# A recurrent mixing layer's preparation and scan, reordered by step, with the state held in PSUM

## What is computed

```
xx = shift(x) - x;  mix = x + xx*maa_x;  lo = tanh(mix @ w1) (4 groups);  xm[g] = x + xx*(lo[g] @ w2[g] + maa[g])
r, k, v, g, w2, kk, a, ma, mk = small projections of xm[0..3], some through tanh or sigmoid
w = -softplus(-(decay + w2)) - 0.5;  kk = k + ..., normalized per head
k = k*(ma + a*(1-ma)) * exp(w*mk);   b = -kk*a;   w = exp(-exp(w))
per head, per step:  s = s*w + (s @ kk)*b + v*k;   y = s @ r
y = groupnorm(y)*ln_w + ln_b + (r*k*faaaa summed per head)*v;   out = (y*g) @ Wo
```

## Time and profile before

| | us |
|---|---|
| median of 3 runs | 2137.53 (2132.94 to 2140.84) |
| the profiled execution, its own time | 2134.84 |
| its span, first to last instruction | 2132.8 |
| `build_projections` | 0 to 69.1 |
| `build_gates` | 69.1 to 166.7 |
| `build_scan` | 166.7 to 336.4 |
| `build_mix_output` | 336.4 to about 450 |
| the six layers and the end | to 2132.8 |

### The profile page before, as it was taken

The page is one execution under the profiler, slowest core; times in us unless marked ns, Lnnn a source line. Parts: engine busy times, 40 slices in busy tenths (PEclk is TensorE's granted clock), DMA queues, the critical chain, the costliest instruction groups (busy, mean ns, idle before and its releaser), DMA issues. The chain is left out here.

```text
span 2132.8 us, 74062 instructions
## 1 busy us (share of the span) xinstructions
PE 1907.6 (89%) x31300; PEld 1318.9 (62%) x31300; DVE 1569.4 (74%) x2888; ACT 1221.0 (57%) x2361; POOL 1161.1 (54%) x682
## 2 busy tenths in 40 slices
PE   6576777948999999999999999999999999999984
PEld 2113556825677766667776776766777677776662
DVE  4768997347787787777877778777787777877743
ACT  4500001126677676776766767667677676776751
POOL 1401221018667666666666767666676666766630
PEclk9788998559999999999999999999999999999996
DMA  1000000033222222322223222232222322322220
GB/s 56 0 0 1 1 0 20 1 128 72 66 67 68 65 72 65 111 66 64 72 69 110 69 64 72 71 105 67 67 72 74 102 68 64 73 63 62 69 53 20
DMA packets 84859, 128.49 MB, mean 60 GB/s; under 512 B 26736, under 2 KB 32304, under 8 KB 83504
## 3 DMA queue, kind: packets, MB, share of 16 engines
q1 hardware_dynamic: 84528, 123.75, 22.8%
HBM read 21.94 MB, written 1.05 MB: 11 GB/s over the span
## 5 line engine op out<-in xcount | busy, mean ns | idle before, releaser
L961 POOL TENSOR_TENSOR qk<-qk,rnorm 128x1024 f32<-128x1024 f32 x192 | 361.4, 1904 | 368.9 <-ACT rnorm L1186 292.6
L955 POOL TENSOR_TENSOR qk<-qk,turnedhalf 128x1024 f32<-128x1024 f32 x192 | 454.8, 2369 | 142.8 <-DVE turnedhalf L1312 142.8
L1308 DVE TENSOR_TENSOR qk<-bank,gains 128x512 f32<-128x512 f32 x384 | 262.2, 683 | 235.1 <-ACT squares L1176 220.6
L1012 PE MATMUL bank<-wqkv,x 128*128 128x512 f32 x768 | 377.8, 595 | 22.0 <-DMA qk_gain<-in_qk_gain 20.1
L1176 ACT ACTIVATE squares<-bank 128x512 f32<-128x512 f32 x384 | 232.6, 606 | 166.0 <-PE bank L1012 163.2
L1312 DVE TENSOR_TENSOR turnedhalf<-bank,gains 128x256 f32<-128x256 f32 x768 | 285.3, 412 | 0.0
L1223 ACT ACTIVATE o_T<-bank 128x512 f32<-128x512 f32 x192 | 104.3, 599 | 229.7 <-PE bank L1076 229.6
L1318 DVE TENSOR_REDUCE rnorm<-squares 128x16 f32<-128x1024 f32 x192 | 230.6, 1201 | 2.8
L1076 PEld LDWEIGHTS bank<-p_T,v_win 64*64 64x64 f32 x12288 | 189.8, 135 | 58.0 <-issue 57.7
L1025 PEld LDWEIGHTS bank<-st_ident,qk 128*128 128x128 f32 x1536 | 179.0, 142 | 58.3 <-issue 52.2
L1017 PE MATMUL bank<-wqkv,x 128*128 128x512 f32 x384 | 202.0, 607 | 7.2 <-DVE turnedhalf L1312 6.7
(11 more groups left out here) (200 smaller groups left out, 3080.9 us busy)
## 6 DMA issues: line engine op xcount, KB each, us to landing
v_win<-v_tok SPq DMA_DIRECT2D x1536, 64.0 KB
wqkv<-in_wqkv SPq DMA_DIRECT2D x6, 1536.0 KB
wo<-in_wo SPq DMA_DIRECT2D x6, 512.0 KB
w<-in_w SPq DMA_DIRECT2D x6, 341.0 KB
w<-in_w SPq DMA_DIRECT2D x6, 192.0 KB
xT_sb<-in_xT SPq DMA_DIRECT2D x1, 1024.0 KB, 5.7
x_tok_sb<-in_x_tok SPq DMA_DIRECT2D x1, 1024.0 KB, 4.8
tables<-in_tables SPq DMA_DIRECT2D x2, 512.0 KB, 4.5
```

Source lines behind the costliest of these rows:

```text
L955: nc.gpsimd.tensor_tensor(out=qk[n % 2][:, half], in0=qk[n % 2][:, half], in1=turnedhalf[:, half], op=ALU.add).then_inc(rot_added.sem, 1)
L961: nc.gpsimd.tensor_tensor(out=by_head(qk[u][:, half]), in0=by_head(qk[u][:, half]), in1=rnorm[u][:, AH * i:AH * (i + 1)].unsqueeze(2).to_b ...
L1012: nc.tensor.matmul(QK_BANKS[i][:, :], shifted_tokens(x, n, P), layer_cols(wqkv, n, 3 * INNER, 512 * i, 512), start=True, stop=True).then_i ...
L1308: nc.vector.tensor_tensor(by_head(qk[u][:, cols]), src, cos.to_broadcast([P, 8, DH]), ALU.mult).then_inc(rotated.sem, 1)
```

## The change

The whole mixing layer is done in step order: the host lays x out by step, so that every tensor of the first phase is already in the order in which the scan reads it. `build_gates` is gone as a phase.

- The projections wait for only three loads first (xT, vecs, w_lo) and for the others before the fifth product. `spread` is no longer loaded. v is projected first in each group, written to DRAM, and read back by SyncE with each row repeated over the 8 rows of its head (16 DMAs for a group of 512, 2 MB in SBUF). GpSimd sums the decays along the steps with 31 additions of 128 x 64. VectorE makes the gain of k by group, with a second sigmoid on ScalarE for 1 - a. g is written turned into token order by ScalarE.
- The rest of the gates' work is made for one group of 8 steps (128 x 512) at a time. Group 0 comes ahead of the first step; groups 1 to 3 are spread as `stages` over the steps of the group before, 9 operations on VectorE, 10 on ScalarE and one product on TensorE for each group. Much of it stays in two PSUM banks, `KK_BANK` and `Z_BANK`.
- The states lie in PSUM banks 4 and 5 and are renewed in place. VectorE makes both products with r out of PSUM. vk is made step by step by GpSimd, two steps ahead (`times_k`), and added by GpSimd to half 0's product with b (`add_vk`); VectorE's `renew0` adds that sum to the state.
- In `build_mix_output` the bonus (line 599) is written turned into token order.

The diff, cut to its core:

```diff
...
-        MAA, FIRST = ("maa0", "maa1", "maa2", "maa3"), ("r", "g1", "xwa", "k", "xk", "v")
-        SECOND = ("g2", "z", "a", "ma", "kk", "mk")
+        MAA, FIRST = ("maa0", "maa1", "maa2", "maa3"), ("v", "r", "g1", "xwa", "k", "xk")
+        SECOND = ("kk", "a", "mk", "ma", "z", "g2")
...
+            for name in FIRST_LOADS:
+                sp.dma_start(t[name][:, :], a[name]).then_inc(loaded_first.sem, 16)
+            for name in rest:
+                sp.dma_start(t[name][:, :], a[name]).then_inc(loaded.sem, 16)
+            for j in range(GROUPS):
+                sp.wait_ge(v_made.sem, j + 1)
+                sp.dma_start(v_dram[:, g_of[j]], t["v"][:, g_of[j]]).then_inc(v_stored.sem, 16)
+                if j == 0:
+                    sp.wait_ge(v_stored.sem, 16)
+                    for h in range(HEADS):
+                        rows = slice(HS * h, HS * (h + 1))
+                        sp.dma_start(v_rep[rows, :, :, :].rearrange("p i l c -> p i (l c)"),
+                                     v_dram[rows, g_of[0]].unsqueeze(0).to_broadcast([HS, HS, GROUP])).then_inc(v_copied.sem, 16)
+            sp.wait_ge(v_stored.sem, 16 * GROUPS)
+            sp.wait_ge(v_copied.sem, 16 * HEADS)
...
+                at, end = max(GROUP * j, CHUNKS), GROUP * (j + 1)
+                nc.vector.tensor_tensor(xx[:, at:end], xT[:, at - CHUNKS:end - CHUNKS], xT[:, at:end], ALU.subtract).then_inc(xx_made.sem, 1)
+                dve.wait_ge(xx_made.sem, 2 * B + j + 1)
...
+                for g in (3, 0, 1, 2):
...
+            def gain(j):
+                gain_j = unheld[:, g_of[j]]
+                dve.wait_ge(a_made.sem, a_made.after(j))
+                dve.wait_ge(ma_made.sem, ma_made.after(j))
+                nc.vector.tensor_tensor(gain_j, gain_j, ma[:, g_of[j]], ALU.mult).then_inc(gain_step.sem, 1)
+                dve.wait_ge(gain_step.sem, gain_step.after(j, 1))
+                nc.vector.tensor_tensor(gain_j, gain_j, t["a"][:, g_of[j]], ALU.add).then_inc(gain_step.sem, 1)
+                dve.wait_ge(gain_step.sem, gain_step.after(j))
+                dve.wait_ge(kk_made.sem, j + 1)
+                nc.vector.tensor_tensor(t["k"][:, g_of[j]], t["k"][:, g_of[j]], gain_j, ALU.mult).then_inc(k_gained.sem, 1)
...
+            def sums(j):
+                pool.wait_ge(z_made.sem, z_made.after(j))
+                for l in range(max(STEPS * j, 1), STEPS * (j + 1)):
+                    if l > 1:
+                        pool.wait_ge(summed.sem, l - 1)
+                    w = [t["w"][:, CHUNKS * m:CHUNKS * (m + 1)] for m in (l - 1, l)]
+                    nc.gpsimd.tensor_tensor(out=w[1], in0=w[0], in1=w[1], op=ALU.add).then_inc(summed.sem, 1)
...
+                    nc.scalar.activation(unheld[:, g_of[j]], bank("a", j)[:, :], ACT.Sigmoid, scale=-1.0,
+                                         bias=vecs[:, V_NAAAAA:V_NAAAAA + 1]).then_inc(a_made.sem, 1)
...
+                    out = t["g"][:, :].rearrange("p (c l) -> p l c", l=CHUNK)[:, STEPS * j:STEPS * (j + 1), :]
+                    nc.scalar.activation(out, bank("g2", j)[:, :].rearrange("p (l c) -> p l c", c=CHUNKS), ACT.Copy).then_inc(g_made.sem, 1)
...
+        def in_step(l, stages):
+            j, s = (l + STEPS) // STEPS, l % STEPS
+            if j < GROUPS:
+                for stage in stages[s]:
+                    stage(j)
...
+            squares(0)
+            absolutes(0)
+            log_z(0)
+            inverse_norm(0)
+            decays(0)
+            key_gain(0)
+            growths(0)
+            decays_again(0)
+            stages = ((squares, absolutes), (log_z, inverse_norm), (decays,), (), (), (key_gain,), (growths,), (decays_again,))
...
+            def renew0(l):
+                if l:
+                    dve.wait_ge(vk_added.sem, l + 1)
+                    nc.vector.tensor_tensor(S_BANKS[0][:, :], S_BANKS[0][:, :], ubvk[:, :], ALU.add).then_inc(s_new[0].sem, 1)
+                else:
+                    dve.wait_ge(vk_made.sem, 1)
+                    nc.vector.tensor_copy(rows(S_BANKS[0][:, :]), vk_of(0)).then_inc(s_new[0].sem, 1)
+            def renew1(l):
+                dve.wait_ge(ub_made[1].sem, l + 1)
+                nc.vector.tensor_tensor(S_BANKS[1][:, :], S_BANKS[1][:, :], ub[:, 1, :], ALU.add).then_inc(s_new[1].sem, 1)
+            def times_r(p, l):
+                dve.wait_ge(s_new[p].sem, l + 1)
+                dve.wait_ge(r_made.sem, l // STEPS + 1)
+                if l >= 2:
+                    dve.wait_ge(y_product.sem, y_product.after(l - 2))
+                nc.vector.tensor_tensor(m2[:, l % 2, :, p, :], rows(S_BANKS[p][:, :]), step(r_step, l), ALU.mult).then_inc(s_r[p].sem, 1)
...
+            soft_sum(0)
+            soft_gate(0)
+            soft_growth(0)
+            unit_kk(0)
+            steps_a(0)
+            times_a(1, 0)
+            gated_kk(0)
+            steps_k(0)
+            steps_b(0)
+            steps_r(0)
+            stages = ((), (), (soft_sum, unit_kk), (soft_gate, gated_kk), (soft_growth, steps_a), (steps_k,), (steps_b,), (steps_r,))
+            for l in range(CHUNK):
+                if l:
+                    times_b(0, l)
+                times_b(1, l)
+                renew1(l)
+                if l + 1 < CHUNK:
+                    times_a(1, l + 1)
+                renew0(l)
+                if l + 1 < CHUNK:
+                    times_a(0, l + 1)
+                times_r(1, l)
+                times_r(0, l)
+                in_step(l, stages)
...
+            def times_k(l):
+                j = l // STEPS
+                pool.wait_ge(k_made.sem, j + 1)
+                if j:
+                    pool.wait_ge(v_copied.sem, v_copied.after(j - 1))
+                nc.gpsimd.tensor_tensor(out=vk_of(l), in0=vk_of(l), in1=step(k_step, l), op=ALU.mult).then_inc(vk_made.sem, 1)
+            def add_vk(l):
+                pool.wait_ge(ub_made[0].sem, l)
+                pool.wait_ge(vk_made.sem, l + 1)
+                if l >= 2:
+                    pool.wait_ge(s_new[0].sem, l)
+                nc.gpsimd.tensor_tensor(out=rows(ubvk[:, :]), in0=rows(ub[:, 0, :]), in1=vk_of(l), op=ALU.add).then_inc(vk_added.sem, 1)
+            for l in range(AHEAD):
+                times_k(l)
+            pool.wait_ge(s_new[0].sem, 1)
+            pool.sem_inc(vk_added.sem, 1)
+            for l in range(CHUNK):
+                if l:
+                    add_vk(l)
+                if l + AHEAD < CHUNK:
+                    times_k(l + AHEAD)
...
-            times_a(0, 0)
-            add_vk(0)
-            times_b(0, 0)
-            renew(0, 0)
-            for l in range(CHUNK):
-                ahead_too = l + 1 < CHUNK
-                times_a(1, l)
-                if ahead_too:
-                    times_a(0, l + 1)
-                if l:
-                    times_r(l - 1)
-                if ahead_too:
-                    add_vk(l + 1)
-                times_b(1, l)
-                if ahead_too:
-                    times_b(0, l + 1)
-                renew(1, l)
-                if ahead_too:
-                    renew(0, l + 1)
-            times_r(CHUNK - 1)
...
+            sums_of_squares(0)
+            product_u(1, 0)
+            stages = ((sums_of_squares,), (), (), (), (), (), (), ())
             for l in range(CHUNK):
-                product_u(1, l)
                 if l + 1 < CHUNK:
+                    product_u(1, l + 1)
                     product_u(0, l + 1)
                 if l:
                     products_y(l - 1)
+                in_step(l, stages)
...
-                nc.vector.tensor_tensor(bonus[:, g_of[j]], banks[4 + j % 2][:, :], t["v"][:, g_of[j]],
+                out = bonus_by_token[:, :].rearrange("p (c l) -> p l c", l=CHUNK)[:, STEPS * j:STEPS * (j + 1), :]
+                nc.vector.tensor_tensor(out, by_step(banks[4 + j % 2][:, :]), by_step(t["v"][:, g_of[j]]),
```

More of the change, by code:

```diff
@@ new lines, in build_scan @@
+        AHEAD = 2
+        vecs = t["vecs"]
+        vk = (v_rep, sb("v_rep1", [P, HS, STEPS, CHUNKS]))
+        decay = sb("decay", [P, CHUNKS + N])
+        sq, relu_z, ka = (sb(n, [P, GROUP]) for n in ("kk_squares", "relu_z", "kk_a"))
+        m, ub = sb("sc_m", [P, 2, W]), sb("sc_ub", [P, 2, W])
+        ubvk = sb("sc_ubvk", [P, W])
+        m2 = sb("sc_m2", [P, 2, HS, 2, CHUNKS])
+        a_step, b_step, r_step, k_step = t["z"], t["mk"], t["r"], t["k"]
+        edged = sig("decay_edged")
+        squared, ss_product, kk_floor, kk_log, kk_norm = sig("kk_squared"), sig("ss_product"), sig("kk_floor"), sig("kk_log"), sig("kk_norm")
@@ L509, in products_y @@
                 for p in range(2):
[L510 removed]
+                    pe.wait_ge(s_r[p].sem, l + 1)
                 if l >= 2:
@@ L1509, in layouts @@
     out["headones"] = same.astype(f)
-    out["spread"] = np.concatenate([(same & (row == i)[:, None]).astype(f) for i in range(HS)], 1)
     out["collect"] = np.concatenate([(same & (row == i)[None, :]).astype(f) for i in range(HS)], 1)
```

465 lines of the change are left out of this document (221 added, 244 removed).

## The result

The changed kernel takes 2066.14 us (median of 4 runs, 2059.89 to 2072.70), the kernel before in the same comparison 2135.24 (median of 4, 2125.82 to 2140.84). The ratio is 0.9681 with a 95% interval of 0.9634 to 0.9728: faster, and 1.9 us from the 2068 that were predicted. The profiled execution took 2064.87 us with a span of 2063.1, 69.7 us shorter than the span before.

What follows compares the result with a forecast made beforehand. Gates were a serial stage and VectorE was full in the scan; preparation and scan -65.4, projections -3.4, bonus +1 gave -67.8 us: 2067.0 from the profiled execution, 2069.7 from the median, said as 2068; range 2057 to 2090.

Steps and rivals of the forecast that it cites:

- Projections: The first phase: 69.1 to 65.7 us, with VectorE starting behind xT, near 6.7.
- Preparation of group 0: Ahead of the first scan step: 12.2 us in place of the gates' 97.6.
- The plain step: Scan step without stages: 5.25 us, 0.28 more than before, set by a loop through TensorE, not by VectorE's list.
- Steps with stages: In the scan, 9 steps of 6.36 us and 9 of 5.76, 14.6 us more in all.
- that mechanism as a rival: TensorE's clock falls in the scan: 31 us more in 18 steps with stages, 2099 us; chance 0.07, 0.01 for all steps.
- The ends: From the last scan step's start: 4.1 us to the last product with r, 2.0 TensorE, 0.5 ScalarE, 2.7 exit.
- The cold start: TensorE starts the scan's phase at half clock: two or three longer steps, 3 us.
- The bonus: In the output phase, written turned into token order: 1 us taken, bounded by 0 and 2.8.
- The write to PSUM: VectorE's results in both renewals and most stage operations: no added cost taken, bounds nothing and 0.15 us an operation.
- slack: In each scan step, GpSimd's addition of vk is hidden and costs from 0.45 us on.
- The v DMAs: Copies of v cost nothing: about 12 us against six scan steps, over 30 us, of cover.
- VectorE held by GpSimd in all operations: In the scan, GpSimd's 2.56 us come on top of each step: 79 us, 2147 us in all; chance 0.04.

Runs made afterwards that it cites:

- the new order: Against the changed kernel, VectorE's list of a step reordered, stages split between two places, TensorE making half 0's product first: 2064.11 us, ratio 0.9683.
- the last experiment: Against the changed kernel, the new order, z produced first of the second set of products, and three more TensorE products a step: 2064.85 us, ratio 0.9672.

## Why the prediction was right

The mechanism came out as forecast: the gates' phase went, a plain step became a loop through TensorE of 5.3 us, the stages filled its wait, and GpSimd stayed hidden. The sum for the part ahead of the layers was -67.8 us, and the profile shows -66.4 + 2.5 = -63.9, 3.9 less. Another 5.8 came from the unchanged layers, so that the total came within 2 us of the forecast (69.7 in the span) is partly luck. The 3.9 are made up below: projections 1.5, steps 1.0, clock 2.1 and output phase 1.5 more than I had, and the cold start 1.7, group 0 0.3 and the end 0.1 less.

- **Projections**, 65.7 predicted, 67.2 measured. The start was better: VectorE at 6.26 for 6.7, the fifth product at 13.93 for 14.4. (The four pairs end at 12.0 by 6.7 + 4 x 1.32, not near 13 as I wrote; the term that went into the sum is the 14.4.) Behind it each of three terms was too small. ScalarE's last operation ended at 60.25 for 59.7: its write of `g_sb` in turned order takes 1.12 us, where I had 0.60. GpSimd's sums ended 3.1 us later for 2.7, at 0.50 each instead of 0.40. The exit with 48 semaphores took 3.87 for 3.3.

```profile
59.10 1.15 ACT L306 ACTIVATE g_sb<-bank 128x512 f32<-128x512 f32 x1
59.39 3.97 POOL L271 TENSOR_TENSOR w_sb<-w_sb 128x64 f32<-128x64 f32 x8 [0.73 <-ACT w_sb L313]
...
67.23 1.28 ACT L388 ACT_TABLE_LOAD   x1 [6.98 <-PEq L83]
```

- **Preparation of group 0**, 12.2 predicted, 11.9 measured (67.23 to 79.73, less the 0.60 by which the first step's product of half 0 with b is left out).
- **The plain step**, 5.25 predicted, 5.30 measured, with each link nearly as given: dependent operations 0.73 or 0.74 apart for 0.72, TensorE's way from 248.30 to 250.21 1.91 for 1.89. With the steps with stages, 13 x 0.05 + 18 x 0.02 is 1.0 us.
- **Steps with stages**, 6.36 and 5.76 predicted, 6.38 and 5.78 measured. The step behind each group cost 0.65 more through the clock, 2 us in all (2.1 with the steps next to them); I had that mechanism as a rival, at 31 us. One of the signs that I gave for a wrong forecast did appear: the granted clock over the steps with stages is 0.92, not 1. What it cost is the 2 us, since in steps with stages the falls were covered. My sum took the clock at 1.00, which did not come true; that the falls cost so little was no part of my argument.
- **The ends.** Last product with r at 264.77 for 4.1 behind the step's start (measured 3.96), ScalarE's end at 267.30, exit 2.7 as said. The cold start cost 1.3 where I had 3 (the first step, counted from 79.13 like the preparation, is 6.61): only that step was long, against the two or three that I took from the earlier trace rows. The bonus takes 1.03 us for each of four operations instead of 0.69, some 1.4 on VectorE. The output phase as a whole was 2.5 us longer, where I had 1. Up to the next phase's table load it took 119.4 us, against 117.4 in the one profile of the kernel before; the thirteen profiles of the changed kernel and its variants lie between 118.5 and 119.9, so at least 1.1 us of it is there in each. What makes it more than VectorE's 1.4 was not looked into.
- **The write to PSUM**, taken at nothing: 0.70 and 0.69 us for lines 533 and 526, where 0.68 is the form's time elsewhere. In a step's six operations on PSUM it is a few hundredths. Line 516 follows line 533 by 0.74 us (246.23 to 246.97), 0.02 over the 0.72 that I had named as a bound; it is inside the 0.05 of the step.
- **GpSimd**: slack 0.45 predicted, 0.6 by experiment. **The v DMAs**: 12 us predicted, 33 measured. This term failed (the landing of 1 MB over 128 partitions was carried over to copies over 8). By the cover that I gave them in the scan, six steps or over 30 us, they would have been late or nearly so. The cover was wider: the copies for groups 2 and 3 are issued at 123.8 and 171.6 us, their packets end at 156.9 and 204.7, and GpSimd's first products with them start at 165.7 and 213.5, so 8.8 us were left. That they stayed off the path is luck.
- The rival **VectorE held by GpSimd in all operations** is refuted, and the experiment with the state in SBUF shows how near it was: with SBUF operands it is 1.50 us a step and 50 us. That PSUM operands keep the two engines apart was a side remark in my prediction, and without it most of the gain is gone.

The Trainium skill, "VectorE: DVE Perf Modes", section on the TRN2 errata, gives an operation out of PSUM a fixed cost of 120 cycles against 58. The runs don't agree here: line 516 took 0.69 us with the state in PSUM and 0.69 with it in SBUF.

## What to carry to other kernels

Where GpSimd works beside VectorE, one of VectorE's operands in PSUM keeps the two from holding each other, and here it was worth 1.50 us in a step of 5.30. Find the limit of a loop by shortening one thing that you think is not the limit: if the time comes back as a wait, the limit is what it waits for. Then look how far behind the next limit stands, here 0.1 us. Where VectorE's work is moved so that TensorE idles more, ask for the clock before the gain is counted: of the 6.6 us of the new order some 2.5 went there. Three spare products a step brought 3.5 us back in the steps of the last experiment and cost 1.5 at the end of the scan, and a gain of the whole isn't shown.
